# Two-layer graph network on one core: the second norm moved behind the last attention weights, and the residual products moved later

## The reference

```python
h0 = x
h = gat_conv(x, edge_index, W1, a_src1, a_dst1, b1, 4, 256, True)     # first attention: 1250 x 1024
h = jax.nn.relu(layer_norm(h, g1, be1)) + (h0 @ Wr1 + br1)            # norm, relu, residual r1
h1 = h
h = gat_conv(h, edge_index, W2, a_src2, a_dst2, b2, 1, 768, False)    # starts with h @ W2
h = layer_norm(h, g2, be2) + (h1 @ Wr2 + br2)                         # residual r2
```

## Time and profile before

| | us |
|---|---|
| median of three timed runs | 877.32 |
| profiled execution, own time | 882.66 |
| its span | 880.9 |
| TensorE busy in the span | 830.4 (94%) |
| VectorE busy | 676.6 (77%) |
| ScalarE busy | 257.1 (29%) |

### The profile page before, as it was taken

How to read it: one execution, slowest core, us unless ns; L and a number is a source line. 1 busy time by engine, 2 the same in 40 slices (tenths; PEclk the granted TensorE clock), 3 DMA queues, 4 the chain that set the end, 5 groups by cost and what they waited for, 6 DMA issues and landing times.

```text
span 880.9 us, 13813 instructions
## 1 busy us (share of the span) xinstructions
PE 830.4 (94%) x5086; PEld 541.3 (61%) x5086; DVE 676.6 (77%) x1188; ACT 257.1 (29%) x455; POOL 60.3 (7%) x82
## 2 busy tenths in 40 slices
PE   2899999899999999998899998999999999999995
PEld 2576777466555444445788887786666566655553
DVE  5988876677676677796979799877975176996686
ACT  3244444500012011113444435533302105770000
POOL 2000000100203000100000010001111000000121
PEclk8799999999999999999899999999999999999998
DMA  8000000414231113335324103112321152212231
GB/s 294 4 2 2 2 2 4 160 43 153 79 130 68 52 46 132 145 119 165 112 67 137 31 31 114 54 54 84 120 82 59 37 197 95 88 57 72 72 108 68
DMA packets 24525, 73.57 MB, mean 84 GB/s; under 512 B 2756, under 2 KB 3676, under 8 KB 24334
## 3 DMA queue, kind: packets, MB, share of 16 engines
q1 hardware_dynamic: 22590, 64.95, 21.4%
q0 software_dynamic: 1872, 7.78, 2.6%
HBM read 52.40 MB, written 20.31 MB: 83 GB/s over the span
## 4 chain that ended last, share of the span: by engine, by line
PE 77%; DVE 15%; issue 3%; DMA 2%; ACT 2%; DVEq 0%; SPq 0%; POOL 0%; POOLq 0%
PE psum L876 18%; PE psum L711 17%; PE psum L903 14%; PE psum L984 11%; PE psum L791 8%; DVE arena L1355 6%; PE psum L740 4%; DVE arena L1487 2%; DVE arena L1502 2%; DMA arena<-as_scratch 1%; ACT arena L991 1%; PE psum L745 1%; PE psum L736 1%; PE psum L891 1%; DVE arena L1443 1%
## 5 line engine op out<-in xcount | busy, mean ns | idle before, releaser
L711 PE MATMUL psum<-arena 128*128 128x512 f16 (+1 forms) x1080 | 229.2, 364 | 2.3 <-DVE arena L1327 1.9
L991 ACT ACTIVATE arena<-psum 128x160 uint16<-128x160 f32 (+6 forms) x226 | 94.7, 466 | 340.3 <-PE psum L711 78.9
L903 PE MATMUL psum<-arena 128*128 128x257 f32 x800 | 180.3, 388 | 11.3 <-ACT arena L1065 9.1
L903 PEld LDWEIGHTS psum<-arena 128*128 128x128 f32 x800 | 154.3, 194 | 36.8 <-ACT arena L1065 11.7
L711 PEld LDWEIGHTS psum<-arena 128*128 128x128 f16 x1080 | 100.6, 98 | 104.5 <-issue 8.1
L876 PE MATMUL psum<-arena 128*128 128x512 f16 x960 | 158.5, 326 | 0.8 <-ACT arena L1065 0.8
L876 PEld LDWEIGHTS psum<-arena 128*128 128x128 f16 x960 | 93.5, 97 | 62.9 <-ACT arena L1065 1.1
L984 PE MATMUL psum<-arena 128*128 128x512 f16 (+2 forms) x600 | 98.4, 325 | 0.0
L1073 ACT ACTIVATE arena<-arena 128x640 f32<-128x640 f32 x80 | 66.1, 831 | 83.8 <-DVE arena L1487 83.8
L1355 DVE CUSTOM_DVE_ANT_0 arena<-arena 128x1280 bf16<-128x1280 bf16 x50 | 71.0, 1489 | 18.9 <-DMA arena<-as_scratch 13.3
L984 PEld LDWEIGHTS psum<-arena 128*128 128x128 f16 x600 | 58.3, 97 | 39.8
(11 more groups left out here) (166 smaller groups left out, 633.1 us busy)
## 6 DMA issues: line engine op xcount, KB each, us to landing
arena<-in_L_gnn_W_dram SPq DMA_DIRECT2D x22, 384.0 KB, 3.2
r_scratch<-arena SPq DMA_DIRECT2D x10, 512.0 KB, 2.6
arena<-uv_scratch SPq DMA_DIRECT2D x16, 320.0 KB, 3.8
arena<-r_scratch SPq DMA_DIRECT2D x10, 512.0 KB, 4.3
x_scratch<-arena SPq DMA_DIRECT2D x10, 384.0 KB, 4.5
arena<-x_scratch SPq DMA_DIRECT2D x10, 384.0 KB, 3.4
r_scratch<-arena SPq DMA_DIRECT2D x10, 384.0 KB, 2.6
arena<-r_scratch SPq DMA_DIRECT2D x10, 384.0 KB, 3.8
```

What stands on the lines that cost most here:

```text
L711: ins = pe.matmul(o[:, a:b], part[:, k, ds(t * P, P)], w[:, k, a:b], start=(not begun and k == 0 and n == 0 and m == 0), stop=(k == kn - 1 ...
L903: last = pe.matmul(p_att[:, ATT_BANKS[ch][j], 0:HID + 1], pf[n % PSLOTS][:, j * P:(j + 1) * P], xl[ch % H][:, k, 0:HID + 1], start=(k == 0 ...
L991: act.activation(out_, in_, ACT.Copy, scale=scale).then_inc(signal, 1)
```

## The change

Tile 1 is no longer normed, transposed and split between the steps of the second half of the first attention; that is now done behind its last weights. `LAYER2` starts with `tr1`; `r` 0 and `r` 1 stand at other places in it, and `tr5` to `tr9` nearer to their own `x`. The lists of ScalarE, VectorE and SyncE follow.

```diff
-NORM_AT = {8: 0, 13: 1}
-TR_AT = {9: 0, 14: 1}
-H1_AT = {15: 0, 20: 1}
+NORM_AT = {8: 0}
+TR_AT = {9: 0}
+H1_AT = {15: 0}
-LAYER2 = ["tr2", "x0", "tr3", "x1", "x2", "tr4", "x3", "tr5", "x4", "tr6", "r0", "x5", "tr7", "r1", "tr8", "x6", "tr9", "x7", "x8", "x9"]
+LAYER2 = ["tr1", "x0", "tr2", "x1", "tr3", "x2", "tr4", "x3", "x4", "tr5", "r0", "x5", "tr6", "x6", "tr7", "r1", "x7", "tr8", "x8", "tr9", "x9"]
...
             residual(2)
-            residual(3)
             weights(3, range(3, KH))
             sp.wait_ge(S["larger_ok"], 2 * H * T)
             weights(4, [0, 1])
+            residual(3)
             residual(4)
             weights(4, [2, 3])
             residual(5)
+            weights(4, [4, 5])
             residual(6)
-            weights(4, [4, 5])
             residual(7)
             weights(4, [6, 7])
...
             evict(2 * H - 1)
+            h1_high(1)
+            xl2_high(0)
             h1_high(2)
             weights(4, [0, 1])
-            xl2_high(0)
+            xl2_high(1)
             h1_high(3)
             weights(4, [2, 3])
-            xl2_high(1)
-            weights(4, [4, 5])
             xl2_high(2)
             h1_high(4)
+            weights(4, [4, 5])
+            xl2_high(3)
             weights(4, [6, 7])
...
+            for t in range(4, T - 1):
                 xl2_high(t)
+                h1_high(t + 1)
+            xl2_high(T - 1)
```

More of the change, by code:

```diff
@@ L1563, in r2_evict @@
                 dve.scalar_tensor_tensor(to, p_x[R2_SLOT[t]][:, 0:D], 1 / WSCALE, xb, ALU.mult, ALU.add).then_inc(S["r2_sb"], 1)
+            norm_start(1)
+            norm_end(1)
             norm_start(2)
+            sums(2 * H - 1)
+            h1_low(1)
             norm_end(2)
-            sums(2 * H - 1)
+            weights(4, [0, 1])
             norm_start(3)
+            xl2_low(0)
             h1_low(2)
             norm_end(3)
-            weights(4, [0, 1])
+            weights(4, [2, 3])
             norm_start(4)
-            xl2_low(0)
+            xl2_low(1)
             h1_low(3)
             norm_end(4)
-            weights(4, [2, 3])
+            weights(4, [4, 5])
             norm_start(5)
-            xl2_low(1)
-            norm_end(5)
-            weights(4, [4, 5])
             xl2_low(2)
             h1_low(4)
-            norm_start(6)
+            norm_end(5)
             weights(4, [6, 7])
-            norm_end(6)
             xl2_low(3)
-            h1_low(5)
             dve.wait_ge(S["par_br2"], 16)
@@ L1591, in _ @@
             steps_done(1)
-            norm_start(7)
+            norm_start(6)
             xl2_low(4)
-            norm_end(7)
-            h1_low(6)
+            h1_low(5)
+            norm_end(6)
             dve.wait_ge(S["dve"], steps_done())
             xb_sum(0)
+            norm_start(7)
+            r2_evict(0)
+            norm_end(7)
+            xl2_low(5)
+            h1_low(6)
             norm_start(8)
-            r2_evict(0)
             norm_end(8)
-            xl2_low(5)
+            xl2_low(6)
             h1_low(7)
@@ L1606, in _ @@
             r2_evict(1)
+            xl2_low(7)
             h1_low(8)
-            xl2_low(6)
+            xl2_low(8)
             h1_low(9)
-            xl2_low(7)
-            xl2_low(8)
             xb_sum(2)
```

## The result

The changed kernel takes 902.99 us, median of four runs (900.51 to 904.58). The kernel before, run beside it, took 879.34 (876.79 to 881.68). The ratio is 1.0267, with a 95% interval of [1.024, 1.0295]. The direction was right; the size was not, and the time lies 3 us above the range's upper end of 900.

A forecast was written before the change was run, and what follows sets the result against it. TensorE, back to back in the second layer, was taken as the bound. Terms 3.15 + 3.15 + 0.70 + 1.9 + 7.0 = 15.9, less 0.46, gave +15.5 us on median 877.32; 0.9 for the clock made 893.7, range 889.0 to 900.0.

The forecast's parts named there:

- What bounds the kernel: TensorE is back to back between 603 and 703 us, so later deliveries by VectorE and ScalarE add to the end.
- Change 1: Turn from channel 4 to 5: norm 1 leaves the first attention, eviction at 530.00, gain 0.46 to 2.3 us, 0.46 taken.
- Rival C: Turn of channel 4: eviction follows the sums, not ScalarE's list; 872.7 us with no second-layer waits; chance 0.02.
- (a): Second layer, tr3: the first Wr2 pair's late cast holds up norm 3 on VectorE; 3.15 us late.
- (b): Second layer, tr4: the second Wr2 pair's cast stands behind h1_high(3), which needs tr3; 3.15 us late.
- (d): Second layer, r0: waits for the last Wr2 pair, loaded after norm 5; 1.9 us, range 0.6 to 2.3.
- (e): Second layer, x6, x8, x9 directly behind their own transposes: TensorE waits 2.34 us three times, 7.0 us.
- Term (c): Second layer, x4: needs h1_low(4), 9.44 us after tr4 starts against 8.74 of TensorE; 0.70 us.
- the clock, "0.9": Clock falls after the two 3.15 us stops; only tr3 and tr4 slow on the path, half of up to 0.87 each: 0.9.
- rival A: Second layer: clock falls after the 2.34 us stops too, three products 1.8 us slower each; 899.1 us, chance 0.19.
- B: Second layer: VectorE's chain does not hold TensorE up, only the 7.0 us of late transposes stays; 883.9 us, chance 0.08.
- D: Second layer: moved work changes nothing on the path, products cover the waits, gain 0.46; 876.9 us, chance 0.05.

The follow-up runs named there:

- kernel with both causes undone: Changed kernel with Wr2 casts earlier in ScalarE's list and tr6, tr8, tr9 one product earlier: 878.3 us, ratio 0.9989.
- without cause 1: Changed kernel with ScalarE's casts of the Wr2 pairs two operations earlier, nothing else: 889.77 us, ratio 1.0123.
- the first experiment: Changed kernel with tr6, tr8 and tr9 each one product earlier, ScalarE's and VectorE's lists following: 891.2 us, ratio 1.0129.
- with the clock held up: Changed kernel with 66 extra matmuls, results unread, in TensorE's six stops of the second layer: 896.74 us, ratio 1.0204.
- the best kernel: Changed kernel with Wr2 casts and tr6, tr8, tr9 earlier, ScalarE's list changed at the turns, 47 extra matmuls: 872.51 us, ratio 0.9907.
- The kernel with late transposes: Kernel before with tr7, tr8 and tr9 each moved directly ahead of its own product: 890.14 us, ratio 1.013.

## Why the prediction was right in direction and wrong in size

**What bounds the kernel: right.** TensorE had no spare time in the second layer, and every late delivery was added to the end. The kernel with both causes undone shows it from the other side: no stops, no loss.

**Change 1: right.** The eviction was forecast at 530.00; it came at 530.21, in a trace whose `tr0` lies 0.22 later. The stop was forecast at 2.48 and is 2.49. Of the two ends for the clock I took the fall, and it fell; that was luck, since the clock held behind the same stop of 2.49 in the two traces of the kernels without cause 1 (shown at the end). Rival C, that the eviction follows the sums, fell with it: the sums came 1.9 us earlier and ScalarE's list held the eviction. Norm 1's new cover held.

**Terms (a), (b), (d), (e): right in place, a little small.** VectorE waits for ScalarE's casts at each pair of Wr2, as the prediction said. These are the first, second and last pair (idle time in brackets; about 5 and 5.5 were forecast for the first and the last; at the third it is 3.86):

```profile
612.54 1.83 DVE L1160 SCALAR_TENSOR_TENSOR arena<-arena 128x768 f16<-128x768 f32 x2 [5.52 <-ACT arena L991]
...
624.75 1.83 DVE L1160 SCALAR_TENSOR_TENSOR arena<-arena 128x768 f16<-128x768 f32 x2 [3.04 <-ACT arena L991]
...
652.67 1.88 DVE L1160 SCALAR_TENSOR_TENSOR arena<-arena 128x768 f16<-128x768 f32 x2 [5.73 <-ACT arena L991]
```

The stops were 3.25 and 3.24 for 3.15, 2.00 for 1.9, 2.46 for 2.34. I added distances of starts, and left out the 0.1 that each idle time was longer and the 0.17 by which the next start is later still. Six stops at 0.25 to 0.3 make 1.7 us. For `r0`, issue to cast was 4.33 us (647.39 to 651.72), in the upper part of the earlier trace rows. The 4.17 was not the one wait in the trace before that ended on such a load, as I had it: the last pair's took 4.37 (626.11 to 630.48). The Trainium skill, "DMA: Bandwidth & Descriptors", section "Anatomy of one DMA", by which the estimate was 2.9 and the term 0.6, is not borne out by this load. It is borne out less by the first experiment, where the second cast of that pair began 6.68 us after the issue (645.80 to 652.48).

**Term (c), 0.70 at `x4`: not seen** in the changed kernel, since a slow `x3` covered it; 0.88 with the clock held up.

**The step that failed is the clock, "0.9".** For `tr3` and `tr4` it was nearly right, though not as argued: the clock fell behind one of the two and not the other, and that fall cost 1.9 less the 0.70 it hid at `x4`, 1.2 for the forecast 0.9; that the two sizes are so near is luck. What was wrong is that the products behind the shorter stops would run at full clock. I had one stop of 2.19 without a fall and one of 2.94 with one, placed 2.34 on the near side (the trace before also has 1.58 without a fall and 3.06 with one, which I left out), and left the other side to rival A with a chance of 0.19. The clock fell behind two of those three stops: 3.3 us. With 1.7 for the stops, 0.3 for `tr4` and 0.2 by which the trace after is later at `tr0`, that is 5.5, the miss against the profiled executions (882.66 + 16.4 = 899.1, measured 904.58).

**The scale.** The miss by medians is 9.3. Of the rest, 2.0 is the median of before, which was 879.34 over four runs and not 877.32 over three, and 1.7 is that the profiled run of before stood 3.3 above its median and the one of after 1.6. The runs of the kernel before spread over 5 us, at least in part because its clock falls differently each time: in the experiments' sessions its fastest run, 876.12, had a mean granted clock of 0.988, and one of 882.1 had 0.980. Such a base is itself uncertain by 2; the range should have had that. Rival A's 899.1 lies 3.9 below the measured median, so three falls instead of none would not have made the size right by themselves.

**Rivals B and D fell:** taking the casts' place back gives 13 us, so VectorE's chain did hold TensorE up; and nothing covered the stops. Of A's three falls two happened.

## What to carry to other kernels

Where TensorE has no idle time, moving a small step in an in-order list is priced by what stands behind it in that list: pairs of casts on ScalarE, put two operations too late, held three norms on VectorE and then TensorE. A product directly behind its own transposes costs the round trip over two other engines and, often, the clock behind it, 3.6 us together here. A stop that can't be removed can be filled with matmuls that nobody reads; that gave back 4 us in the layer's profile and 6 by the medians, and in the best kernel, beside shorter stops, five runs lay within 0.9 us.

## What was not expected of the hardware

The length of a stop did not decide whether the granted clock fell. In the profile after, it fell behind stops of 2.46 (twice), 2.49 and 3.24, and stayed behind 2.46 and 3.25. The kernel with late transposes kept it behind the 2.94 at the turn, behind which the kernel before lost it; TensorE's row there:

```profile
528.67 10.67 PE L903 MATMUL psum<-arena 128*128 128x257 f32 x48 [2.94 <-ACT arena L1065]
```

Nor did length and place together decide it. Up to channel 5 the changed kernel and four of its variants are the same program with the same stop of 2.49 at the turn: the clock fell behind it in the changed kernel, in the one without cause 2 and in the one with 66 extra matmuls, and held in the one without cause 1 and in the one with both undone. The row without cause 1, beside 23.63 us for the changed kernel's 100 matmuls:

```profile
528.75 21.94 PE L903 MATMUL psum<-arena 128*128 128x257 f32 x100 [2.49 <-ACT arena L1065]
```

Yet it was not mere chance everywhere: of the three stops of 2.46 that stand directly ahead of a product, the clock fell behind the first and the third and held behind the second in all four traces that have them unfilled. What decides it stays open. Shown is only that the clock held where the stops were filled, and that the idle times left there (up to 0.88 us) lost none.
